# The opening loads of an attention and FFN kernel, issued from one engine's queue or from two

## The reference

```python
xn = layernorm(x)                                   # no gain, no bias
q, k, v = xn @ wq.T + bq, xn @ wk.T + bk, xn @ wv.T + bv
attn = softmax(q @ k.T * 256 ** -0.5)
lora = up_aux @ (lora_up @ (lora_down @ down_aux))  # ranks 4, 100 and 50
out = x + attn @ v + xn @ (W + lora).T + b
```

## Time and profile before

| | |
|---|---|
| median of three runs | 508.9 us |
| the profiled execution's own time | 509.78 us |
| its span in the trace | 507.9 us |
| PE busy | 502.6 us, 99% of the span |
| POOL, DVE, ACT busy | 379.4, 364.6, 278.7 us |
| PE's share of the chain that ended last | 98% |
| read from HBM and written to it | 16.54 MB and 8.39 MB |

### The profile page before, as it was taken

The page is one execution under the profiler, slowest core; times in us unless marked ns, Lnnn a source line. Parts: engine busy times, 40 slices in busy tenths (PEclk is TensorE's granted clock), DMA queues, the critical chain, the costliest instruction groups (busy, mean ns, idle before and its releaser), DMA issues.

```text
span 507.9 us, 8231 instructions
## 1 busy us (share of the span) xinstructions
PE 502.6 (99%) x3003; PEld 448.8 (88%) x3003; DVE 364.6 (72%) x822; ACT 278.7 (55%) x594; POOL 379.4 (75%) x229
## 2 busy tenths in 40 slices
PE   8999999999999999999999999999999999999997
PEld 6888988989899898998989899898998989899897
DVE  4889976958488586876768666796748758386594
ACT  4758872574726738166573647547474553724450
POOL 5878939886699966997869968799679976671730
PEclk9999999999999999999999999999999999999999
DMA  8120032010320105010050100501011010100102
GB/s 247 66 84 2 1 89 119 1 42 1 115 93 1 41 1 206 2 43 0 1 207 2 43 1 1 206 2 41 1 61 64 3 43 0 43 0 2 43 5 79
DMA packets 8105, 25.45 MB, mean 50 GB/s; under 512 B 872, under 2 KB 3202, under 8 KB 7170
## 3 DMA queue, kind: packets, MB, share of 16 engines
q1 hardware_dynamic: 7914, 24.93, 13.7%
q10 hardware_dynamic: 152, 0.00, 0.0%
HBM read 16.54 MB, written 8.39 MB: 49 GB/s over the span
## 4 chain that ended last, share of the span: by engine, by line
PE 98%; DVE 1%; ACT 0%; POOL 0%; issue 0%; POOLq 0%
PE o_ps L1224 12%; PE o_ps L1223 12%; PE o_ps L1222 11%; PE g_ps L1094 10%; PE g_ps L1095 10%; PE g_ps L1096 10%; PE s_ps L1094 9%; PE s_ps L1095 9%; PE s_ps L1096 9%; PE s_ps L1268 1%; PE o_ps L1094 1%; PE o_ps L1096 1%; PE o_ps L1095 1%; PE g_ps L1166 0%; PE s_ps L1224 0%; PE s_ps L1223 0%
## 5 line engine op out<-in xcount | busy, mean ns | idle before, releaser
L540 POOL TENSOR_TENSOR p_lo<-s,p_hi 128x1024 fp32r<-128x1024 f32 x60 | 143.9, 2425 | 39.4 <-ACT p_hi L714 39.3
L707 ACT ACTIVATE s<-s,e 128x512 f32<-128x512 f32 x128 | 84.3, 714 | 117.4 <-DVE s L944 117.4
L1224 PE MATMUL o_ps<-v_lo,p_hi 128*128 128x256 f32 x480 | 136.1, 283 | 0.0
L1223 PE MATMUL o_ps<-v_hi,p_lo 128*128 128x258 f32 x480 | 135.1, 282 | 0.0
L1222 PE MATMUL o_ps<-v_hi,p_hi 128*128 128x258 f32 x480 | 134.6, 281 | 0.0
L1222 PEld LDWEIGHTS o_ps<-v_hi,p_hi 128*128 128x128 f32 x480 | 91.3, 190 | 1.8
L1223 PEld LDWEIGHTS o_ps<-v_hi,p_lo 128*128 128x128 f32 x480 | 91.1, 190 | 1.6
L1224 PEld LDWEIGHTS o_ps<-v_lo,p_hi 128*128 128x128 f32 x480 | 90.2, 188 | 0.0
L903 DVE SCALAR_TENSOR_TENSOR tile_max<-s_ps,e,tile_max 128x512 f32<-128x512 f32 x80 | 59.9, 749 | 34.1 <-PE s_ps L1096 32.6
L1094 PE MATMUL s_ps<-xt_hi,zt_hi 128*128 128x512 f32 x192 | 74.9, 390 | 0.0
L1096 PE MATMUL s_ps<-xt_hi,zt_lo 128*128 128x512 f32 x192 | 74.7, 389 | 0.0
(11 more groups left out here) (165 smaller groups left out, 1003.2 us busy)
## 6 DMA issues: line engine op xcount, KB each, us to landing
out<-base SPq DMA_DIRECT2D x15, 512.0 KB, 2.6
x_sb<-in_L_attn_x SPq DMA_DIRECT2D x7, 1024.0 KB, 8.2
x_t<-in_x_t SPq DMA_DIRECT2D x6, 1024.0 KB, 6.3
x_sb<-in_L_attn_x SPq DMA_DIRECT2D x4, 256.0 KB, 5.5
out<-base SPq DMA_DIRECT2D x4, 128.0 KB, 1.9
s<-in_L_attn_wk SPq DMA_DIRECT2D x1, 258.0 KB, 4.1
s<-in_L_attn_wq SPq DMA_DIRECT2D x1, 256.0 KB, 4.9
s<-in_L_attn_wv SPq DMA_DIRECT2D x1, 256.0 KB, 5.2
```

The lines of the kernel that those rows point to most:

```text
L540: nc.gpsimd.tensor_tensor(p_pair(g, p_lo_sb, j), s_pair(j), p_pair(g, p_hi_sb, j).bitcast(f32), ALU.subtract).then_inc(p_lo_made, 1)
L707: nc.scalar.activation(s[:, n, :], s[:, n, :], ACT.Exp, bias=e[b % 2][:, n:n + 1]).then_inc(p_made, 1)
L1223: nc.tensor.matmul(o[:, 0:D + ONES], lo, v_hi[i][:, n, 0:D + ONES], start=False, stop=False)
L1224: mm = nc.tensor.matmul(o[:, 0:D], hi, v_lo[i][:, n, :], start=False, stop=last)
```

## The change

The loads of wk, the lora factors, wq and wv are issued by ScalarE, in this order, behind bq; SyncE issues x's four pieces first, then down_aux and the rest. TensorE turns the identity only 18 times, at the start; the first lora product stands behind the one for `e_row`; the second (`mid_rank_mm`) stands behind `first_v(1)`. ACT, DVE and POOL are reordered to match: ACT normalizes tile 0 before it copies the first lora product, copies the second one behind `first_v_hi(1)`, makes `turned_hi(0)` before tile 2, and `first_v_hi(1)` before `z_bias`. DVE makes the low part of `a` before the statistics of the last two tiles. POOL begins its first `make_first_prod` only when the low part of wv is made.

```diff
         WARM, WARM_ON = 18, 5   ->   WARM = 18
 # sync
             load_first(0)
-            sp.dma_start(wk_sb, rows(wk_bk)).then_inc(wk_loaded, DMA)
             load_first(1)
-            sp.dma_start(down_aux_sb, down_aux).then_inc(down_aux_loaded, DMA)
-            sp.dma_start(wq_sb, rows(wq)).then_inc(wq_loaded, DMA)
-            sp.dma_start(wv_t_sb, rows(wv_t)).then_inc(wv_loaded, DMA)
             load_first(2)
             load_first(3)
+            sp.dma_start(down_aux_sb, down_aux).then_inc(down_aux_loaded, DMA)
             sp.dma_start(wq_t_sb, rows(wq_t)).then_inc(wq_t_loaded, DMA)
 # gpsimd
             pool.wait_ge(e_row_made, 1)
-            pool.wait_ge(first_xn_made, 2)
+            pool.wait_ge(wv_lo_made, 1)
             make_first_prod(0, 0)
 # scalar
             act.dma_start(bq_col[:, :], bq_in).then_inc(bq_loaded, DMA)
+            act.dma_start(wk_sb, rows(wk_bk)).then_inc(wk_loaded, DMA)
             act.dma_start(lora[:, :], lora_in).then_inc(lora_loaded, DMA)
+            act.dma_start(wq_sb, rows(wq)).then_inc(wq_loaded, DMA)
+            act.dma_start(wv_t_sb, rows(wv_t)).then_inc(wv_loaded, DMA)
...
+            make_xn(0)
             act.wait_ge(rank_mm, 1)
             nc.scalar.activation(rank_t, ...).then_inc(rank_made, 1)
-            make_xn(0)
-            act.wait_ge(mid_rank_mm, 1)
-            nc.scalar.activation(mid_rank, ...).then_inc(mid_rank_made, 1)
             act.wait_ge(wv_loaded, DMA)
             nc.scalar.activation(vf_hi[:, :, 0:D], wv_t_sb, ACT.Copy).then_inc(wv_hi_made, 1)
+            turned_hi(0)
             make_xn(2)
-            turned_hi(0)
             turned_hi(1)
             act.wait_ge(a_mm, 1)
             nc.scalar.activation(a_hi[:, :, :], ...).then_inc(a_hi_made, 1)
             first_v_hi(0)
+            first_v_hi(1)
+            act.wait_ge(mid_rank_mm, 1)
+            nc.scalar.activation(mid_rank, ...).then_inc(mid_rank_made, 1)
             act.wait_ge(wq_bk_made, 1)
             ...                                    # z_bias, two activations
-            first_v_hi(1)
             make_xn(4)
 # vector
             turned_lo(1)
-            dve.wait_ge(x0_loaded[3], DMA)
-            make_stats(0, range(6, TILES))
-            make_mean_var(0, range(4, TILES))
             dve.wait_ge(a_hi_made, 1)
             ...                                    # a_lo
+            dve.wait_ge(x0_loaded[3], DMA)
+            make_stats(0, range(6, TILES))
+            make_mean_var(0, range(4, TILES))
             first_v_lo(0)
 # tensor
             pe.wait_ge(identity_made, 1)
             ...                                    # 18 transposes of the identity
-            pe.wait_ge(lora_loaded, DMA)
-            nc.tensor.matmul(o_ps[1][0:DDIM, 0:UDIM], lora_down, lora_up_t, ...).then_inc(rank_mm, 1)
-            turn_identity(WARM_ON)
             pe.wait_ge(bq_spread, DT)
             pe.wait_ge(wk_loaded, DMA)
             ...                                    # the product for e_row
-            pe.wait_ge(down_aux_loaded, DMA)
-            pe.wait_ge(rank_made, 1)
-            nc.tensor.matmul(o_ps[1][0:UDIM, D:2 * D], rank_t, down_aux_sb, ...).then_inc(mid_rank_mm, 1)
+            pe.wait_ge(lora_loaded, DMA)
+            nc.tensor.matmul(o_ps[1][0:DDIM, 0:UDIM], lora_down, lora_up_t, ...).then_inc(rank_mm, 1)
...
             first_v(0)
             first_v(1)
+            pe.wait_ge(down_aux_loaded, DMA)
+            pe.wait_ge(rank_made, 1)
+            nc.tensor.matmul(o_ps[1][0:UDIM, D:2 * D], rank_t, down_aux_sb, ...).then_inc(mid_rank_mm, 1)
             first_z(0)
```

More of the change, by code:

```diff
@@ L296, in attention_plus_lora_ffn @@
         FIRST_FFN_BANKS = (o_ps[0], o_ps[1], o_ps[0], o_ps[1])
-        WARM, WARM_ON = 18, 5
+        WARM = 18
         def group_bank(k):
@@ L724, in _ @@
                   .then_inc(bq_spread, 1)
+            make_xn(0)
             act.wait_ge(rank_mm, 1)
             nc.scalar.activation(rank_t, o_ps[1][0:DDIM, 0:UDIM], ACT.Copy).then_inc(rank_made, 1)
-            make_xn(0)
-            act.wait_ge(mid_rank_mm, 1)
-            nc.scalar.activation(mid_rank, o_ps[1][0:UDIM, D:2 * D], ACT.Copy).then_inc(mid_rank_made, 1)
             act.wait_ge(wv_loaded, DMA)
             nc.scalar.activation(vf_hi[:, :, 0:D], wv_t_sb, ACT.Copy).then_inc(wv_hi_made, 1)
+            turned_hi(0)
             make_xn(2)
-            turned_hi(0)
             turned_hi(1)
@@ L737, in _ @@
             first_v_hi(0)
+            first_v_hi(1)
+            act.wait_ge(mid_rank_mm, 1)
+            nc.scalar.activation(mid_rank, o_ps[1][0:UDIM, D:2 * D], ACT.Copy).then_inc(mid_rank_made, 1)
             act.wait_ge(wq_bk_made, 1)
@@ L1263, in last_p_times_v @@
                     mm.then_inc(pv_mm, 1)
-            def turn_identity(times):
-                for _ in range(times):
-                    nc.tensor.transpose(s_ps[2][:, 0:PT], identity[:, :], identity[:, :])
             pe.wait_ge(identity_made, 1)
-            turn_identity(WARM)
-            pe.wait_ge(lora_loaded, DMA)
-            nc.tensor.matmul(o_ps[1][0:DDIM, 0:UDIM], lora_down, lora_up_t, start=True, stop=True).then_inc(rank_mm, 1)
-            turn_identity(WARM_ON)
+            for _ in range(WARM):
+                nc.tensor.transpose(s_ps[2][:, 0:PT], identity[:, :], identity[:, :])
             pe.wait_ge(bq_spread, DT)
@@ L1280, in _ @@
             mm.then_inc(e_row_mm, 1)
-            pe.wait_ge(down_aux_loaded, DMA)
-            pe.wait_ge(rank_made, 1)
-            nc.tensor.matmul(o_ps[1][0:UDIM, D:2 * D], rank_t, down_aux_sb,
-                             start=True, stop=True).then_inc(mid_rank_mm, 1)
+            pe.wait_ge(lora_loaded, DMA)
+            nc.tensor.matmul(o_ps[1][0:DDIM, 0:UDIM], lora_down, lora_up_t, start=True, stop=True).then_inc(rank_mm, 1)
             def make_a(d):
@@ L1298, in _ @@
             first_v(1)
+            pe.wait_ge(down_aux_loaded, DMA)
+            pe.wait_ge(rank_made, 1)
+            nc.tensor.matmul(o_ps[1][0:UDIM, D:2 * D], rank_t, down_aux_sb,
+                             start=True, stop=True).then_inc(mid_rank_mm, 1)
             first_z(0)
```

## The result

The changed kernel takes 514.15 us (median of 4 runs, 513.6 to 514.51) against 508.88 for the kernel before: ratio 1.0095, interval 1.0083 to 1.0108. It is slower by 5.3 us; 509.4 was predicted, with 510.9 as the upper end. The profiled execution took 514.10 us with a span of 512.2, so it is 4.32 us longer than the profiled one of before (509.78).

What follows compares the result with a forecast made beforehand. TensorE, never idle once first_v(0) starts, was taken as the bound. That start 0.2 us earlier, 0.56 for the second lora product and 0.1 for ties made +0.46, rounded to +0.5: 509.4 us, range 507.9 to 510.9.

Steps and rivals of the forecast that it cites:

- What bounds the kernel: TensorE never stops once first_v(0) starts, so only that start and the work behind it count, us for us.
- F: Start of first_v(0) on TensorE, 11.99 us in the kernel before, forecast at 11.8.
- S: Start of the first scores on TensorE, 19.76 us in the kernel before, forecast at F + 8.33.
- The landing of wv: Arrival of the wv load in the opening, 8.24 us in the kernel before, taken as 9.5.
- even sharing of bytes: Case in which both load queues get equal bytes: wv lands at 8.96 us, F is 11.3, sum -0.1 us.
- one packet each: Case in which the two load queues alternate packet by packet: wv lands at 10.33 us.
- The landing of wq: Arrival of wq in the opening, put at 7.55 us or later, giving TensorE's own floor for F of 10.4.
- From W to F: Way from wv's landing through ACT's copy, high part and normalized tiles, then TensorE's transposes, to F: 2.3 us.
- Rival C: TensorE falls to half pace in the opening's gaps: +2.7 us, half of it +1.3, so 510.2 to 511.6; chance 0.12.
- rival B: Packets alternate and x takes two thirds: wv lands at 10.33, F is 12.6, +1.3 us, 510.2; chance 0.2.
- The second lora product behind F: This product moves on TensorE from ahead of F to behind it, where it is never hidden: +0.56 us.
- the ties: TensorE reaches the first scores about when ACT's and DVE's inputs are ready: 0.1 us charged, between 0 and 0.5.

Runs made afterwards that it cites:

- after again: The changed kernel run a second time with nothing changed: 513.84 us, ratio 1.0095 to the kernel before.
- e2: The changed kernel with its loads put back on SyncE's queue in the old order, all else as changed: 509.36 us, ratio 1.0011.
- e3: The changed kernel with 26 instead of 18 identity transposes at the start and 13 more behind the first lora product: 512.99 us, ratio 1.0076.
- e5: The changed kernel with x's first pieces loaded as eight 128 KB loads with 1 KB rows instead of four with 2 KB rows: 509.95 us, ratio 1.0020.
- after: The changed kernel itself, with the whole diff against the kernel before: 514.15 us, ratio 1.0095.
- e4: The changed kernel with the tiny loads, bq and the lora factors, issued by SyncE behind x's first piece: 511.74 us, ratio 1.0053.
- e8: e4 with 26 instead of 18 identity transposes at the start: 511.08 us, ratio 1.0043.

## Why the prediction was wrong

- **What bounds the kernel**: right. PE without a pause from F on, and a us on S is a us at the end.
- **The landing of wv (W = 9.5)**: this is the step that failed. wv landed at 12.53, a term short by 3.0 of the 3.8 us by which the profiled execution missed its own forecast of 510.3. The forecast took a value between even sharing of bytes (8.96) and one packet each (10.33). The second came nearest: by 10.5 us 957 of the 968 packets of ScalarE's queue had been moved. It left out two things. It counted 48 packets an engine for the weights and put those of bq and lora at "1 KB" and "2 KB"; by packets they are 152 of 968 on that queue and stand at its head. If each cost a packet of x of 2 KB, an estimate, they are 304 KB, 0.83 us at 367 KB a us, and W is 11.2. And a landing is that of the last packet: from 10.5 to 12.5 us 11 packets of ScalarE's queue were still moved, beside 368 of SyncE's, and the semaphore waited for them (18 packets in after again, with W = 12.03). Why these came so late is open. That bytes were no measure could be seen in the earlier trace rows, 35 packets against 53 with hardly a byte in them; I read that row as pricing nothing.
- **The landing of wq**: the sum never moved it. PE's floor for F, 10.4, was worked out from wq at 7.55, its landing in the kernel before; it landed at 10.0. At full pace the floor would be 12.95 (10.08 + 0.97 + 0.44 + 0.86 + 0.6), earlier than W + 2.06 = 14.59; at half pace it was 15.22, and that is what F was.
- **From W to F (2.3 us)**: right where PE is at full pace and x is there in time, 2.06 to 2.48 in e2, e3 and e5; 2.69 in after, where PE's half pace set F. The low part of wv took 0.69 as taken, but the 1.1 us thought to be won with it were lost in only one of the two profiles of the kernel before.
- **Rival C (half pace, 0.12)** was set against the forecast and rival B as if one excluded the others. It came with them: half pace followed on a gap that a late weight had left, on the second one in after (1.5 us) and on the first in after again (1.25 us). In after it is worth 0.6 + 0.16 us in the profile, between e4 and e8 1.9. Its price in the prediction is off by itself: 8.5 us from 6 on make F = 14.5 and not 14.
- **The second lora product behind F (0.56) and the ties (0.1)**: together 0.97 measured in e2, and 0.75 in e8. In e2 `first_v(1)` starts 0.15 us late for DVE's low part, and 0.09 and 0.07 go as PE enters and leaves the product. The last turn ahead of the first scores takes 0.35 us to their start in e2 as in before: that tie, the one that was charged, cost nothing. The tie at `first_v(1)` was named in the prediction and cost the 0.15.
- **The reorder alone**, worth -0.8 by the sum at the old loads, is +0.34 (1.0011) measured in e2; in the profiles it is 0.46 better than one execution of before and 0.17 worse than the other. The 0.8 were measured from an execution that had lost the race.
- **Sum**, by the profiles of before and after: W is 4.29 later, the way from W to F 1.06 shorter (2.69 against 3.75), the way from F to S 1.13 longer (0.97 and 0.16). Together this is 4.36, for 4.32 measured.
- **The rule on bandwidth**: the Trainium skill, DMA: Bandwidth & Descriptors, section "Issuing engines are not separate DMA queues", says that a second issuing engine brings no bandwidth. The trace agrees: 242 GB/s over the first 12 us against 245.

## What to carry to other kernels

Count packets beside bytes when two queues feed the same DMA engines: here the queue with the shorter rows lost, and tiny loads of many rows held back whatever stood behind them. Work out the landing of every load that moves, not only of the last one needed. Keep what the critical path waits for on one queue in order of need, or cut the competitor's rows to the same length. Where a wait may open a gap on TensorE in the opening, price the half pace together with the wait, and take two profiles before a single row of 1.80 us carries a term.

## What was not expected of the hardware

Halving x's packets at the same bytes, with twice the issues, brought wv 2.9 us earlier (12.03 to 9.13) and bq's landing from 3.8 to 2.5 us after issue. The same loads in the same lists landed wv at 12.5, 12.0, 12.0 and 11.1 us in four profiles. The granted clock can read 1.00 while PE is at half pace: e4 has 1.00 over 10 to 12 us with a half of `a` at 1.86 us, where after has 0.50 and the same duration. After again reads 1.00 from start to end, with e_row at 2.06 us against 1.04 in before, and before reads 1.00 over the first transposes, at 0.23 us each against 0.11 in `turn(0)`. The record seems to miss some changes of the clock, so the pace is safer read from a duration known at both levels.
